# A fused graph layer pair: the weighted sums spread over eight units, and the tail's steps moved by a unit

## The reference, cut to what matters

```
hi = x @ W1[:128];  hj = x @ W1[128:]
h  = relu(hi[i] + hj[j] + b1)            # for every pair (i, j): 128*128 vectors of 128
y  = layernorm(h @ W2 + b2) * gamma + beta
x1 = layernorm(x + sum_j adj[i, j] * y[i, j])
Wh = x1 @ Ww.T + Wb;  si = Wh @ aw[:128];  sj = Wh @ aw[128:]
e  = exp(si[i] + sj[j] + ab) * adj[i, j]
out = layernorm(x1 + (e / e.sum(j)) @ x1)
```

## Time and profile before

| | us |
|---|---|
| median of 3 runs | 2819.02 (2816.72 to 2820.27) |
| profiled execution | 2814.19 |
| its span | 2811.0 |
| TensorE (PE) busy | 2541.0 (90%) |
| ScalarE busy | 2209.3 (79%) |
| VectorE busy | 2120.4 (75%) |
| GpSimd busy | 2006.4 (71%) |

### The profile page before, as it was taken

How to read it: one execution, slowest core, us unless ns; L and a number is a source line. 1 busy time by engine, 2 the same in 40 slices (tenths; PEclk the granted TensorE clock), 3 DMA queues, 4 the chain that set the end, 5 groups by cost and what they waited for, 6 DMA issues and landing times.

```text
span 2811.0 us, 77120 instructions
## 1 busy us (share of the span) xinstructions
PE 2541.0 (90%) x21263; PEld 2145.4 (76%) x21263; DVE 2120.4 (75%) x17817; ACT 2209.3 (79%) x3841; POOL 2006.4 (71%) x1227
## 2 busy tenths in 40 slices
PE   8998998988989889898898988988989889898897
PEld 7787777777877778777787777877777777777785
DVE  7777777777777777777777777777777777777776
ACT  7787777777777778777787777877778777787785
POOL 7777777777777677776777677777777677776774
PEclk9999999999999999999999999999999999999999
DMA  0000000000000000000000000000000000000000
GB/s 19 7 6 11 10 5 10 5 10 10 5 10 5 10 10 5 10 8 8 10 5 10 10 5 10 5 10 10 5 10 6 10 10 5 10 9 6 10 4 9
DMA packets 48051, 23.49 MB, mean 8 GB/s; under 512 B 6208, under 2 KB 47808, under 8 KB 47808
## 3 DMA queue, kind: packets, MB, share of 16 engines
q1 hardware_dynamic: 46512, 21.12, 2.7%
q10 hardware_dynamic: 1296, 0.20, 0.0%
HBM read 17.11 MB, written 4.19 MB: 8 GB/s over the span
## 4 chain that ended last, share of the span: by engine, by line
PE 62%; DVE 15%; ACT 11%; issue 10%; ACTq 0%; POOL 0%; DVEq 0%; DMA 0%
PE y_ps L527 44%; PE agg_ps L571 13%; DVE squares L515 10%; ACT y L270 6%; ACT h L288 4%; DVE q L515 2%; PE prep_ps L527 1%; DVE o_sb L451 1%; PE att_ps L527 1%; PE tail_ps L527 1%; PE tail_ps L582 1%; ACT att_ps L351 1%; DVE eT L485 0%; ACT ln_v L317 0%; DVE tail_ps L433 0%
## 5 line engine op out<-in xcount | busy, mean ns | idle before, releaser
L259 POOL TENSOR_TENSOR h<-bT,aT 128x1024 f32<-128x1024 f32 x1024 | 1937.0, 1913 | 771.8 <-PE y_ps L527 756.5
L515 DVE CUSTOM_DVE_ANT_0 squares<-y_ps,y 128x128 bf16<-128x128 f32 x8192 | 1865.3, 286 | 612.9 <-ACT y L270 590.2
L527 PE MATMUL y_ps<-w_pair,h 128*128 128x128 f32 x16384 | 2001.4, 283 | 4.0 <-DVE w_back L421 2.3
L527 PEld LDWEIGHTS y_ps<-w_pair,h 128*128 128x128 f32 x16384 | 1946.8, 198 | 68.4 <-DVE q L515 48.8
L270 ACT ACTIVATE y<-y_ps 128x508 f32<-128x508 f32 x2048 | 1142.8, 599 | 413.4 <-PE y_ps L527 403.7
L288 ACT ACTIVATE h<-h 128x1024 f32<-128x1024 f32 x1024 | 1092.5, 1067 | 9.8 <-POOL h L259 9.8
L515 DVE DVE_READ_ACCUMULATOR2_ANT q<- 128x1 f32 x8192 | 678.3, 83 | 0.0
L571 PE MATMUL agg_ps<-y,wz 128*32 128x512 f32 x4096 | 466.0, 595 | 0.0
L571 PEld LDWEIGHTS agg_ps<-y,wz 128*32 128x32 f32 x4096 | 119.9, 109 | 245.3 <-issue 229.8
L582 PE MATMUL tail_ps<-ident,o_sb 128*128 128x128 f32 x64 | 22.7, 354 | 196.3 <-DVE o_sb L451 196.3
L582 PEld LDWEIGHTS tail_ps<-ident,o_sb 128*128 128x128 f32 x64 | 9.4, 147 | 209.8 <-DVE o_sb L451 209.8
(11 more groups left out here) (90 smaller groups left out, 699.2 us busy)
## 6 DMA issues: line engine op xcount, KB each, us to landing
x_in<-in_x_dram SPq DMA_DIRECT2D x64, 64.0 KB, 2.0
adj_in<-in_adj_dram SPq DMA_DIRECT2D x64, 64.0 KB, 2.0
x_res<-in_x_dram SPq DMA_DIRECT2D x64, 64.0 KB, 1.9
adj_res<-in_adj_dram SPq DMA_DIRECT2D x64, 64.0 KB, 1.9
out_dram<-x_out SPq DMA_DIRECT2D x64, 64.0 KB, 1.5
w<-in_L_gnn_W_dram ACTq DMA_DIRECT2D x1, 64.0 KB, 2.4
w1a<-in_L_gnn_W_dram SPq DMA_DIRECT2D x1, 64.0 KB, 2.2
w1b<-in_L_gnn_W_dram SPq DMA_DIRECT2D x1, 64.0 KB, 2.3
```

The lines of the kernel that those rows point to most:

```text
L259: nc.gpsimd.tensor_tensor(h[:, u % HRING].rearrange("k (r g) s -> k r g s", g=GROUPS), bT[:, p, :].unsqueeze(1).unsqueeze(1).broadcast_to( ...
L515: last = nc.vector.tensor_tensor_reduce(out=squares[:, k % YRING, n, :], in0=y_ps[k % YRING][:, n, :], in1=y[:, p, i, :], scale=1.0, scala ...
L527: return nc.tensor.matmul(dst, lhsT, rhs, start=start, stop=stop)
```

## The change

The weighted sums stand one chunk at a time behind the units 4, 6, 7, 9, 10, 12, 13 and 15. Tail steps move: o_sb on VectorE from unit 1 to unit 0, with adj_sum behind it in unit 1; its transpose on TensorE from 2 to 3, the product with w_back from 4 to 5, prep products from 8 to 9, the score transpose from 9 to 10; on ScalarE ln_v and rstd from 0 to 1, ln1 and rs1 from 6 to 7; on VectorE eT from 11 to 10, the second normalisation from 13 to 12 and from 15 to 14; on GpSimd x_beta from 7 to 6. No instruction is added or dropped.

```diff
-    POOL_WEIGHTS_UNIT, POOL_RESIDUAL_UNIT = 5, 7
-    BURST = {7: range(0, CHUNKS // 2), UNITS - 1: range(CHUNKS // 2, CHUNKS)}
+    POOL_WEIGHTS_UNIT, POOL_RESIDUAL_UNIT = 5, 6
+    SUM_AT = {u: c for c, u in enumerate((4, 6, 7, 9, 10, 12, 13, 15))}
...
 # ScalarE
-                    if gather and u == 0:
+                    if gather and u == 1:
                         act.wait_ge(v_ready, t)
...
-                    if tail and u == 6:
+                    if tail and u == 7:
                         act.wait_ge(mv1_ready, t - 1)
...
 # VectorE
-                    if tail and (u, e) == (0, 1):
+                    if tail and (u, e) == (1, 0):
                         dve.wait_ge(xres_loaded[p], nth16(half, p, -2) * 2)
...
-                    if tail and (u, e) == (1, 0):
+                    if tail and (u, e) == (0, 0):
                         dve.wait_ge(agg_done, (t - 1) * CHUNKS)
...
-                    if tail and u == 1 and 1 <= e < CHUNK:
+                    if tail and u == 0 and 1 <= e < CHUNK:
...
-                    if tail and (u, e) == (11, 0):
+                    if tail and (u, e) == (10, 0):
                         dve.wait_ge(ex_ready, t - 1)
...
 # TensorE
-                    if tail and u == 2:
+                    if tail and u == 3:
                         pe.wait_ge(o_stored, t - 1)
...
-                    if tail and u == 4:
+                    if tail and u == 5:
                         pe.wait_ge(oT_sb_s, t - 1)
...
-                    if tail and u == 9:
+                    if tail and u == 10:
                         pe.wait_ge(si_cols_ready, t - 1)
...
-                    if gather and u in BURST:
-                        for chunk in BURST[u]:
-                            if chunk == 0:
-                                pe.wait_ge(w_ready, t)
-                                if early >= 2:
-                                    pe.wait_ge(o_stored, t - 1)
-                            weighted_sums(1 - p, chunk)
+                    if gather and u in SUM_AT:
+                        if SUM_AT[u] == 0:
+                            pe.wait_ge(w_ready, t)
+                            if early >= 2:
+                                pe.wait_ge(o_stored, t - 1)
+                        weighted_sums(1 - p, SUM_AT[u])
```

More of the change, by code:

```diff
@@ L485, in slot @@
                         nc.vector.tensor_tensor(eT[:], ex, adjS[:, p, :], ALU.mult).then_inc(eT_ready, 1)
-                    if tail and (u, e) == (13, 0):
+                    if tail and (u, e) == (12, 0):
                         dve.wait_ge(att_done, t - 1)
                         nc.vector.reciprocal(rz[:], att_ps[:, K:K + 1]).then_inc(rz_ready, 1)
-                    if tail and (u, e) == (13, 1):
+                    if tail and (u, e) == (12, 1):
                         dve.wait_ge(rz_ready, t - 1)
@@ L493, in slot @@
                                                        op0=ALU.mult, op1=ALU.add).then_inc(x2p_ready, 1)
-                    if tail and (u, e) == (13, 2):
+                    if tail and (u, e) == (12, 2):
                         dve.wait_ge(x2p_ready, t - 1)
                         nc.vector.bn_stats(st2[:], x2p).then_inc(st2_ready, 1)
-                    if tail and (u, e) == (13, 3):
+                    if tail and (u, e) == (12, 3):
                         dve.wait_ge(st2_ready, t - 1)
@@ L501, in slot @@
                         nc.vector.bn_aggr(mv2[:], st2[:]).then_inc(mv2_ready, 1)
-                    if tail and (u, e) == (15, 0):
+                    if tail and (u, e) == (14, 0):
                         dve.wait_ge(rs2_ready, t - 1)
@@ L587, in slot @@
                         prep_transposes(t + 1, 1 - p, nth16(half, p, 1), True)
-                    if prep and u == 8:
+                    if prep and u == 9:
                         prep_products(t + 1)
-                    if tail and u == 9:
+                    if tail and u == 10:
                         pe.wait_ge(si_cols_ready, t - 1)
```

## The result

| | before | after |
|---|---|---|
| median, us | 2818.0 (2816.7 to 2820.3) | 2630.6 (2629.6 to 2630.9) |
| ratio | | 0.933, 95% interval 0.932 to 0.935 |
| span of the profiled execution | 2811.0 | 2627.4 |

A forecast was written before the change was run, and what follows sets the result against it. TensorE, busy 90%, was taken as the bound, idling for o_sb and eT and losing 84 us to low clock. Terms -132 - 63 - 15 - 74 + 84 = -200 gave 2614, on the median's scale 2620; range 2565 to 2715.

The forecast's parts named there:

- stall in units 12 to 15: Short TensorE stall on the PSUM ring, 0.25 us a slot, goes since two groups now stand between: 15 us gained.
- Edit 2: TensorE's o_sb wait: moving tail steps leaves shorter ring stalls, 213 us before, 81 after, gain 132 (0 to 210).
- Edit 5: TensorE's clock: with shorter stands only 10 of the 84 us lost at the low level remain, gain 74 (0 to 84).
- Edit 3: TensorE's wait for eT goes, with eT one unit earlier and the score transpose one later: gain 63 us (40 to 63).
- Edit 4: Remaining moves (x_beta on GpSimd, ln1, prep products, rz to x_out on VectorE): priced 0; without cover, 25 us.
- Edit 1: Sums one group at a time on TensorE: 384 more width changes at 0.22 us cost 84 us (0 to 250).
- The sign that the prediction gave: Lone groups on TensorE, from their start to the next products: 1.08 us if right, 1.5 or 1.2 if wrong.
- rival 2: Drain at each TensorE width change, 0.34 us in place of 0.22: +46 us, 2665; chance 0.12.
- rival 1: Ahead of unit 0 a lone group's pause is too short; ring stalls return, clock falls: +26, 2845, slower; chance 0.06.
- 3 (clock at pass starts): TensorE's clock still falls at loop starts, where stands of 1.4 and 0.4 us are close: about +40, 2660; chance 0.16.
- 4: A lone group on TensorE loses one round, 0.65 us a change: +165 us, 2785; chance 0.05.
- 5: Better: half the group edges hidden (-42) and the stalls a third smaller (-25): 2555; chance 0.10.

The follow-up runs named there:

- the filled wait: Eight more matmuls (16 instructions) put ahead of TensorE's wait for o_sb, against the kernel before: 2755.0 us, ratio 0.976 to 0.979.
- behind 5 and 12: Tail steps moved, the two bursts of sums behind units 5 and 12 instead of 7 and 15: 2654.7 us, ratio 0.940 to 0.943.
- matmuls between: One more full-width matmul between each two chunks of a burst, against the kernel with steps moved and two bursts: 2736.7 us, ratio 0.970 to 0.973.

## Why the prediction was right, and where its terms were off

The mean slot went from 43.57 to 40.59 us (first start of the o_sb transpose to the 62nd: 94.76 to 2752.59 before, 94.11 to 2569.77 after, each over 61). Taken apart by start-to-start times, as a mean of a slot within a pass and one at its start; the last term is what the slot takes without any stall, 37.55 before and 39.40 after, us a slot:

| term | forecast | measured |
|---|---|---|
| o_sb wait against ring stalls | -2.13 | 3.40 to 1.19: -2.21 |
| eT wait | -1.01 | -1.00 |
| stall in units 12 to 15 | -0.25 | -0.25 |
| clock | -1.19 | -1.30 |
| width changes | +1.35 | +1.85 |
| sum | -3.23 | -2.91 (slot: -2.98) |

The clock term is worked out from the granted clock (80 us over 62 slots); the filled wait shows that about 1.1 us of the 1.30 came as time, and the rest is what is named there, the hidden 0.17 us and the pace of the low level.

**Edit 2, the o_sb wait: right**, in place, in what came next, and in size (0.67 and 1.70 us for 0.7 and 1.9). The undoing of o_sb and of ln_v each shows it. VectorE's and TensorE's half of the o_sb move were undone together, so what each is worth is open. That ln_v had to move too was in the walk, and is now shown: 66 us.

**Edit 5, the clock: right.** Behind the stalls that are left, at most 1.2 us of idle, the low level is granted in no slot with products, so the 10 us that the prediction left did not occur either. The filled wait shows the mechanism by itself.

**Edit 3, eT: right in the trace, but the move may not have been needed.** The wait is gone, but the spreading alone removes it as well. The prediction put it down to moves and group together; either would have done, and the changed kernel with eT late was not run. With bursts kept the move is worth 33 us.

**Edit 4, the remaining moves**, priced at 0, was not tested by itself.

**Edit 1, the width changes: mechanism right, the term mis-sized.** The step that was off: "first round and exit cost 0.13, with the entry's 0.10 about 0.22". A third part of 0.10 stands behind the first full-width instruction after the sums. It was in the trace before, and I had read past it: behind a burst the two prep products took 0.33 us to the next where they take 0.22 now. The term should have been 384 x 0.33 = 128 us instead of 84. (The slots without products have nearly no changes, so the trace has 380 more and not 384.) In the table it is 1.85 and not 2.0 since restarts after a wait had a similar 0.1 that went with the waits.

So this term alone was short by 62 x 0.50 = 31 us, and the time missed by 11. The other terms came out better by 5 us (o_sb wait) and 7 (clock), some 4 us of the slot are in no term, and the step from the profiled execution to the median was 1.0 us and not 4.8. These have nothing to do with the width changes. That the time came within 11 us is partly luck.

The sign that the prediction gave would not have shown it: it asked for a lone group of 1.08 us from its start to the next products, and of 1.2 if rival 2 held. Measured are 1.00. The entry's 0.10 lies ahead of that stretch and the missed 0.10 behind it; only the distance from group to group, 2.98 where 2.64 is the pace, shows the whole.

It is rival 2's number, 0.34, though split otherwise than rival 2 had it. The Trainium skill's rule that a change of tiling mode drains the engine (TensorEngine Tiling (Array Packing), section Tiling Modes) gives no price. The trace agrees with it so far that there is a cost at each change, here 0.33 us for in and out with these shapes; whether a drain is the reason no run here shows.

**Rivals.** 1 (the pause goes, the wait stays) did not occur; its mechanism exists: taking the pause ahead of unit 0 away (behind 5 and 12) costs 128 us, though not the whole 210 that rival 1 spoke of. 2 had the price of a change right, 0.33 to 0.34, and its time, 2665, wrong, for the reasons just given. 3 (clock at pass starts) did not occur. 4 is out: 0.33, not 0.65. 5 is out.

What the prediction did not ask is whether the two halves belong together. They do not: the moves are worth 2818 - 2527 = 291 us, the spreading costs 104 of them (and 149 in the kernel before, where it lengthens the o_sb wait).

## What to carry to other kernels

Where one engine waits for a step of another, move producer and consumer apart until the wait in the buffer ring comes first; then look at what holds the ring, which here was a small step (ln_v) standing ahead of copies it had nothing to do with. Time a change in two halves: here one half took 10.3% off the time and the other put 3.7% back. With the steps moved the sums in one, two, three, four and eight bursts gave 2590, 2527, 2557, 2543 and 2631 us: few changes of width are cheaper, but where the pauses stand counts as much (2655 for two bursts elsewhere), and here one is needed ahead of the slot's start.

## What the runs showed of the hardware

- A change from full-width to four-strip matmuls and back costs 0.33 to 0.34 us with these shapes, in three readings: 2.98 for 2.64 us in the trace after, 1.41 for 1.08 in the trace with matmuls between, and 128.0 us over 378 changes between two timed kernels.
- TensorE runs 16 more instructions a slot and the kernel is 63 us faster, when they are put into its wait. In the kernel before the low level was granted behind 17 of 34 stands of 2.5 us and behind all 28 of 3.7 to 4.3 us (mean clock 0.68 over the 5.30 us of one such stretch); with the wait filled, behind none of 34 stands of 0.7 us and behind 3 of 28 stands of 2.0 to 2.5 us.
- In a low stretch a product instruction starts every 0.2135 us, at the high level every 0.1115.
- VectorE loses on average 1.9 to 2.1 us at each start of a loop pass but the first (53.9 to 58.8 us in 28 waits in all fourteen kernels). On TensorE no such idle time appears: 1331.85 in the kernel with two bursts is a pass start and runs at pace.
